# Last layer of a fused four-layer kernel: scores and value mix as three split terms each, with their inputs rounded early in a batch

## The chip, the cores and the metric

The kernel runs on 1 core of one Trainium2 chip. The time is that of the device for one execution of the whole program, in microseconds (us). Lower is better. The change touches the last of three stages of the program; the two stages before it are the same instructions in both kernels.

## What is computed

Four layers act one after the other on `x` of 32 batches, 256 positions and 256 channels. The last two are done in one stage of the kernel, batch by batch, and this is the part of the reference that the change is about:

```
# layer L2: a feed-forward layer with a shared part and an expert chosen per batch
h = gelu(x @ W1 + b1)                       # 256 -> 1024
x = x + concat([h @ W2 + b2, h @ We[indices] + be[indices]], -1)    # 192 + 64 columns
# layer L3: attention of a batch on the tensor `key` (also its value)
q = x + braak_embed[braak_stages][..., None]
attn = softmax(einsum('bsd,btd->bst', q, key), axis=-1)
x = x + einsum('bst,btd->bsd', attn, value)
```

## The kernel before, in words

The whole of `x` stays on the chip, transposed, in `x_all` (128 partitions, 2 chunks of channels, 32 batches of 256 columns). The stage in question is `expert_and_final`, whose tiles and semaphores all begin with `c_`. Each engine has its own instruction list, written out by hand as a `body(n, par, ...)` for batch `n`; batches 2 to 29 run in a hardware loop with two bodies in it (even and odd), and the first two and last two batches are written out. Nothing is scheduled by a planner: the order in each list is the order on that engine, and semaphores tie the lists together.

Matrix products with the feed-forward weights are done in three terms: each operand is split into a rounded part (`_hi`, type fp32r) and the rest (`_lo`, the difference), and high x high, high x low and low x high are summed. The two products of the attention, scores (`c_pS`, L1820) and value mix (`c_pV`, L1837), use plain fp32 operands instead, four matmuls each.

For each batch the work on the engines is this:

- TensorE (PE): `hidden(n+1, r)`, r = 0 to 3, 12 matmuls each into `c_pH`; `output(n, r)`, 12 matmuls each, all into the one accumulator `c_pO`; `scores(n-1)`; four transposes of the probabilities (`turn`, `c_pT`); and `mix_values(n-1)`. The order of a body is hidden 0, scores, output 0, hidden 1, output 1, hidden 2, turn, output 2, hidden 3, output 3, mix.
- ScalarE (ACT): `hidden` (gelu of `c_pH` into `c_hid`), `exps` (exponentials of the scores with the row maximum as bias, and their sums), `turned` (copy of `c_pT`), `high_x` and `expert_high` (rounded parts). Gelu and exponential need different tables, so each batch has two table loads.
- VectorE (DVE): `split` (rounded part and rest of `c_hid`), `maxima`, `normalize`, `low_x`, `residual` (adds `c_pO` to `x_all`), `queries` (adds the embedding), `final` (adds `c_pV` to `x_all`, into `c_y`).
- GpSimd (POOL): `expert_low` (the rest of the expert weights, `c_w2b_lo`, L1611) and the DMA that stores `c_y`.
- SyncE (SP): the loads of expert weights, biases, embedding, key and value for the next batch.

Links that the prediction follows: `output(n, 0)` waits for `residual(n-1)`, since there is one `c_pO`; `residual(n)` waits for `output(n, 3)`; `scores(n)` waits for `queries(n)`; `maxima(n)` for `scores(n)`; `exps(n)` for `maxima(n)`; `mix_values(n)` for `turned(n)`; `split(n, r)` for gelu r of the batch.

Of the kernel before, what the change touches and what calls it, by code (L numbers as in the profile page):

```python
# [1473 lines left out]
def expert_and_final(nc, sem_ctx, ctx, t, X, NB, consts):  # L1474
# [36 lines left out]
    hid_lo = [sb(f"hid_lo{i}", [P, 2, S], F32R) for i in range(ROUNDS)]  # L1511
    query = sb("query", [P, C, S])
    neg_max = sb("neg_max", [P, C])
# [3 lines left out]
    prob_t = sb("prob_t", [P, C, S])  # L1517
# [8 lines left out]
    d_w1, d_b1, d_w2, w_hi, w_lo = (sem(n) for n in ("d_w1", "d_b1", "d_w2", "w_hi", "w_lo"))  # L1526
    xhi_done, xlo_done, ehi_done, elo_done = (sem(n) for n in ("xhi", "xlo", "ehi", "elo"))
    hid_mm, gelu_done, hhi_done, hlo_done, out_mm, x3_done = (sem(n) for n in ("hid_mm", "gelu", "hhi", "hlo", "out_mm", "x3"))
    query_done, s_mm, max_done, exp_done, inv_done, prob_done = (sem(n) for n in ("query", "s_mm", "max", "exp", "inv", "prob"))
    t_mm, pt_done, v_mm, y_done = (sem(n) for n in ("t_mm", "pt", "v_mm", "y"))  # L1530
# [11 lines left out]
    LOADS = 7  # L1542
    block = ctx.enter_context(nc.Block())

# [11 lines left out]
    @block.sync  # L1556
    def _(sp):
        sp.dma_start(w1[:], t["w1"].rearrange("(k p) e -> p k e", p=P)).then_inc(d_w1, 16)
        sp.dma_start(b1[:], t["b1"]).then_inc(d_b1, 16)
        sp.dma_start(w2[:], t["w2"].rearrange("(k p) e -> p k e", p=P)).then_inc(d_w2, 16)  # L1560
        sp.dma_start(expert_i[:], t["expert"]).then_inc(d_in, 16)
        sp.dma_start(stage_i[:], t["stage"]).then_inc(d_in, 16)
        for i in range(2):
            sp.dma_start(b2[i][:, 0:1], t["b2"][0:P]).then_inc(d_in, 16)
            sp.dma_start(b2[i][0:SHARED - P, 1:2], t["b2"][P:SHARED]).then_inc(d_in, 16)
        sp.dma_start(embed_all[:], t["embed"].partition_broadcast(P)).then_inc(d_in, 16)
        sp.wait_ge(d_in, 16 * LOADS)

        def load(n, par):
            at = slice(n, n + 1) if isinstance(n, int) else bass.ds(n, 1)  # L1570
            expert = sp.value_load(expert_i[0:1, at], min_val=0, max_val=EXPERTS - 1)
            stage = sp.value_load(stage_i[0:1, at], min_val=0, max_val=STAGES - 1)
            if not (isinstance(n, int) and n < 2):
                sp.wait_ge(elo_done, n - 1)

            sp.dma_start(we[par][:], t["we"][bass.ds(expert, 1)].rearrange("o p k e -> p (o k) e")).then_inc(d_exp[par], 16)
            if not (isinstance(n, int) and n < 2):
                sp.wait_ge(x3_done, n - 1)
            sp.dma_start(b2[par][SHARED - P:P, 1:2], t["be"][bass.ds(expert, 1)].rearrange("o p f -> p (o f)")).then_inc(d_bias[par], 16)
# [22 lines left out]
    def _(pool):  # L1602
# [18 lines left out]
        loop(pool, body)  # L1621
        store(NB - 1, 1)
# [4 lines left out]
    def _(dve):  # L1627
# [21 lines left out]
        def queries(n, par):  # L1649
            dve.wait_ge(x3_done, n + 1)  # L1650
            dve.wait_ge(d_emb[par], landed(n, par))
            at_least(dve, s_mm, n)
# [56 lines left out]
        loop(dve, body)  # L1709
        maxima(NB - 1)  # L1710
        normalize(NB - 1)
        final(NB - 1, 1)

    @block.scalar
    def _(act):
# [6 lines left out]
        def expert_high(n, par):  # L1722
# [3 lines left out]
            act.activation(w2b_hi[par][:, :, SHARED - P:P], we[par][:], ACT.Copy).then_inc(ehi_done, 1)  # L1726
# [17 lines left out]
        def turned(n):  # L1744
            act.wait_ge(t_mm, n + 1)
            at_least(act, v_mm, n)
            act.activation(prob_t[:], pT[:], ACT.Copy).then_inc(pt_done, 1)

        def body(n, par, ahead, splits, has_3):
            if ahead:  # L1750
                hidden(n + 1, 0)
            if has_3:
                exps(n - 1)
            if ahead:
                hidden(n + 1, 1)
                hidden(n + 1, 2)
            if has_3:
                turned(n - 1)
            if splits:
                high_x(n + 2, par)  # L1760
            if ahead:
                expert_high(n + 1, 1 - par)
                hidden(n + 1, 3)

# [10 lines left out]
        act.wait_ge(d_b1, 16)  # L1775
        for r in range(ROUNDS):
            hidden(0, r)
        expert_high(0, 0)
        loop(act, body)
        exps(NB - 1)  # L1780
# [3 lines left out]
    def _(pe):  # L1784
# [15 lines left out]
        def output(n, par, r):  # L1800
            pe.wait_ge(hlo_done, ROUNDS * n + r + 1)
            if r == 0:
                pe.wait_ge(elo_done, n + 1)
# [10 lines left out]
        def scores(n, par):  # L1814
            pe.wait_ge(query_done, n + 1)
            pe.wait_ge(d_key[par], landed(n, par))
            at_least(pe, exp_done, n)
            for m in range(C):
                for k in range(C):
                    ins = pe.matmul(pS[:, m], query[:, k, m * P:m * P + P], key_t[par][:, k], start=(k == 0), stop=(k == C - 1))  # L1820
            ins.then_inc(s_mm, 1)

        def turn(n):
            pe.wait_ge(prob_done, C * (n + 1))
            at_least(pe, pt_done, n)
# [5 lines left out]
        def mix_values(n, par):  # L1831
            pe.wait_ge(pt_done, n + 1)
            pe.wait_ge(d_val[par], landed(n, par))
            at_least(pe, y_done, n)
            for m in range(C):
                for k in range(C):
                    ins = pe.matmul(pV[:, m], value[par][:, k, m * P:m * P + P], prob_t[:, k], start=(k == 0), stop=(k == C - 1))  # L1837
            ins.then_inc(v_mm, 1)

        def body(n, par, ahead, splits, has_3):  # L1840
            if ahead:
                hidden(n + 1, 1 - par, 0)
            if has_3:
                scores(n - 1, 1 - par)
            output(n, par, 0)
# [3 lines left out]
            if ahead:  # L1849
                hidden(n + 1, 1 - par, 2)  # L1850
            if has_3:
                turn(n - 1)
            output(n, par, 2)
# [3 lines left out]
            if has_3:  # L1857
                mix_values(n - 1, 1 - par)
# [4 lines left out]
        loop(pe, body)  # L1863
        scores(NB - 1, 1)
# [103 lines left out]
```

## Time and profile before

| | |
|---|---|
| time, median of 3 runs | 1984.78 us (1984.0 to 1987.01) |
| profiled execution: its own time, its span | 1988.33 us, 1986.4 us |
| granted TensorE clock over the span, as a share of full | 0.969 |
| busy over the span | PE 93%, DVE 75%, ACT 59%, POOL 33% |
| last stage | from about 1467 us to the end |

The busy shares are means over three stages that have different limits; the stage that the change touches has to be read by itself, in a stretch of it. Matmul records overlap, since they are pipelined: what a group of matmuls costs is read from start to start, not from the duration of a record. The profiled execution took 3.55 us more than the median.

### The profile page before, as it was taken

What the parts mean: (1) busy time and instruction counts of PE and PEld (TensorE: products, weight loads), DVE (VectorE), ACT (ScalarE), POOL (GpSimd) and SP (SyncE); (2) the same over time, 40 slices, a digit from 0 to 9 for tenths busy, and PEclk for the clock granted to TensorE, in tenths of its full rate; (3) what the DMA queues carried; (4) which work ended last, traced back from release to release, by engine and by line L of the source; (5) the groups of instructions that cost most, each with busy time, mean ns of one, the idle gap of its engine ahead of it and who ended that gap; (6) DMA issues with size and microseconds to landing.
All of it is one profiled execution on the core that took longest, in us unless ns stands there. A gap on an engine that the chain in (4) does not pass through costs nothing. (4 is left out here: it accounts for less than half of the span.)

```text
span 1986.4 us, 43323 instructions
## 1 busy us (share of the span) xinstructions
PE 1839.2 (93%) x14542; PEld 1452.8 (73%) x14542; DVE 1485.8 (75%) x2206; ACT 1180.6 (59%) x2458; POOL 664.7 (33%) x655
## 2 busy tenths in 40 slices
PE   5899999999999994499999999999949999999997
PEld 4565555555555552388888888888849999999997
DVE  6888888888888892787878777787736666666664
ACT  1676667666666662366666666666545555555563
POOL 3244444444444442433343434333301111111111
PEclk9999999999999996699999999999979999999998
DMA  3333333333333320100000000000022222222221
GB/s 94 102 125 105 114 116 123 110 109 118 118 119 106 112 94 27 30 1 0 0 0 0 0 0 0 0 0 0 0 91 62 71 71 82 85 71 71 79 88 46
DMA packets 104940, 126.16 MB, mean 64 GB/s; under 512 B 27840, under 2 KB 70464, under 8 KB 104896
## 3 DMA queue, kind: packets, MB, share of 16 engines
q1 hardware_dynamic: 86912, 102.72, 16.3%
q0 software_dynamic: 17408, 22.61, 3.8%
q8 instruction: 25, 0.41, 0.1%
q10 hardware_dynamic: 576, 0.26, 0.1%
q14 instruction: 19, 0.16, 0.0%
HBM read 56.54 MB, written 9.44 MB: 33 GB/s over the span
## 5 line engine op out<-in xcount | busy, mean ns | idle before, releaser
L409 DVE TENSOR_REDUCE a_top<-a_s 128x4 f32<-128x1024 f32 x256 | 309.1, 1209 | 88.5 <-PE a_s L646 88.4
L509 ACT ACTIVATE a_e<-a_t 128x512 f32<-128x512 f32 x512 | 276.6, 592 | 147.7 <-PE a_t L660 143.2
L419 DVE SCALAR_TENSOR_TENSOR a_e<-a_e,a_w_t 128x1024 f32<-128x1024 f32 x256 | 328.1, 1282 | 6.3 <-ACT a_e L509 6.3
L1733 ACT ACTIVATE c_hid<-c_pH,c_b 128x256 f32<-128x256 f32 x256 | 107.4, 471 | 190.1 <-PE c_pH L1796 189.7
L926 POOL TENSOR_TENSOR b_decayed<-b_table,b_mod_t 128x1024 f32<-128x1024 f32 x64 | 118.8, 1876 | 211.3 <-ACT b_mod_t L1198 211.3
L1357 PE MATMUL b_pS<-b_gated_t,b_decayed 128*128 128x256 f32 x768 | 183.8, 389 | 1.0
L675 PE MATMUL a_v<-a_e,a_v_pad 128*32 128x256 f32 x2048 | 165.4, 396 | 8.8 <-DVE a_e L419 6.9
L641 PE MATMUL a_s<-a_absent,a_eye 64*128 64x512 bf16 x1024 | 157.1, 386 | 6.7 <-DMA a_absent<-a_absent 5.4
L1796 PE MATMUL c_pH<-c_x_hi,c_w_hi 128*128 128x256 f32 x512 | 150.8, 294 | 12.5 <-DVE c_w_lo L1698 12.4
L1357 PEld LDWEIGHTS b_pS<-b_gated_t,b_decayed 128*128 128x128 f32 x768 | 142.3, 192 | 23.8 <-issue 6.7
L646 PE MATMUL a_s<-a_st 63*128 63x256 f32 x1024 | 152.5, 377 | 0.0
L1611 POOL TENSOR_TENSOR c_w2b_lo<-c_we,c_w2b_hi 128x512 fp32r<-128x512 f32 x32 | 54.6, 1706 | 280.0 <-ACT c_w2b_hi L1726 280.0
L1796 PE MATMUL c_pH<-c_x_hi,c_w_lo 128*128 128x256 f32 x512 | 146.2, 286 | 0.0
L1796 PE MATMUL c_pH<-c_x_lo,c_w_hi 128*128 128x256 f32 x512 | 145.6, 284 | 0.0
L1065 DVE TENSOR_TENSOR b_inner<-b_inner,b_prod 128x448 f32<-128x448 f32 (+6 forms) x224 | 128.0, 571 | 22.7
L1637 DVE CAST c_hid_hi<-c_hid 128x512 fp32r<-128x512 f32 x128 | 54.5, 426 | 114.6 <-PE c_pO L1810 93.2
L1048 DVE TENSOR_TENSOR b_state<-b_pS,b_w_rep 128x512 f32<-128x512 f32 x128 | 85.3, 687 | 65.5 <-PE b_pS L1357 65.5
L646 PEld LDWEIGHTS a_s<-a_st 63*128 63x128 f32 x1024 | 99.1, 190 | 37.8 <-issue 1.4
L262 POOL TENSOR_TENSOR a_split<-a_full,a_split 128x512 fp32r<-128x512 f32 x64 | 91.8, 1435 | 61.0 <-DVE a_e L419 36.8
L660 PE MATMUL a_t<-a_st 64*128 64x256 f32 x1024 | 108.0, 290 | 4.2 <-ACT a_e L509 2.8
L1796 PEld LDWEIGHTS c_pH<-c_x_hi,c_w_hi 128*128 128x128 f32 x512 | 98.8, 193 | 13.9 <-DVE c_w_lo L1698 12.8
L641 PEld LDWEIGHTS a_s<-a_absent,a_eye 64*128 64x128 bf16 x1024 | 29.4, 95 | 108.1 <-issue 87.7
(253 smaller groups left out, 5152.3 us busy)
## 6 DMA issues: line engine op xcount, KB each, us to landing
a_st<-a_split SPq DMA_DIRECT2D x384, 128.0 KB, 2.2
a_xs<-in_xT SPq DMA_DIRECT2D x32, 256.0 KB, 2.7
x_all<-in_xT SPq DMA_DIRECT2D x32, 256.0 KB, 3.6
a_r_rep<-a_r_rows POOLq DMA_DIRECT2D x64, 128.0 KB, 3.7
c_we<-in_we SPq DMA_DIRECT2D x32, 256.0 KB, 2.7
c_key_t<-in_keyT SPq DMA_DIRECT2D x32, 256.0 KB, 3.2
c_value<-in_key SPq DMA_DIRECT2D x32, 256.0 KB, 2.7
out<-c_y POOLq DMA_DIRECT2D x32, 256.0 KB, 3.3
```

What stands on the lines that cost most here:

```text
L409: dve.tensor_reduce(top[:, qc, half].rearrange("p (r j c) -> p r j c", r=2, j=2)[:, :, cc], ps_s[g % 2][:], AX.X, ALU.max)\
L419: dve.scalar_tensor_tensor(out=buf[:], in0=buf[:], scalar=BIG, in1=w_t[par][:, kc].unsqueeze(1).to_broadcast([P, 4, S]), op0=ALU.min, op1= ...
L509: act.activation(e[g % E_BUFS][:, 2 * r:2 * r + 2], ps_t[r][:], ACT.Exp).then_inc(exp_done, 1)
L641: pe.matmul(ps_s[g % 2][:, r], eye[par][rows, hq], absent2[rows, qc, hq].unsqueeze(1).to_broadcast([64, C, S]), start=(hq == 0), stop=Fals ...
L646: ins = pe.matmul(ps_s[g % 2][:, r, c], st[par][rows, 0, j, c, qc * P:qc * P + P], st[par][rows, 1, j, c], start=False, stop=(c == C - 1), ...
L660: ins = pe.matmul(ps_t[r][:, c], st[par][rows, 1, j, c, kc * P:kc * P + P], st[par][rows, 0, j, c], start=True, stop=True, tile_position=( ...
L675: ins = pe.matmul(ps_v[32 * j:32 * j + 32, cc], v_pad[par][:, kc, 4 * (2 * cc + half) + j], e[g % E_BUFS][:, j], start=(g % 4 == 0), stop= ...
L926: ins = pool.tensor_tensor(decayed[par][:, lo:lo + cnt], table[:, lo:lo + cnt], mod_t[:, k].unsqueeze(1).to_broadcast([P, cnt, TRACES]), A ...
L1065: dve.tensor_tensor(y, y, pr, ALU.add).then_inc(inner_done, 1)
L1357: ins = pe.matmul(pS[q % 2][:, i], decayed[par][:, lo:lo + 4].rearrange("p a d -> p (a d)"), gated_t[par][:, k], start=(k == 0), stop=(k = ...
L1733: ins = act.activation(hid[r % 2][:, i], pH[r][:, i], ACT.Gelu, bias=b1[:, 2 * r + i:2 * r + i + 1])
L1796: ins = pe.matmul(pH[r][:, i], w[:, k, m * P:m * P + P], x[par][:, k], start=(w is w1_hi and x is x_hi and k == 0), stop=(x is x_lo and k ...
```

## The change

Scores and value mix are now done in three terms, like the other products: `product` issues 12 matmuls for each, high x high, low x high and high x low. Their operands have to be split first: key and value into `key_p` and `value_p` (rounded on ACT, rest on POOL), query into `query_p` (rounded on ACT, rest on DVE), and the transposed probabilities into two `prob_t` (rounded on ACT, rest on DVE). The orders of the lists are written anew. On PE the value mix of batch n-2 now stands ahead of `output(n, 0)`, and scores of n-1 behind it. The roundings `high_x`, `high_query` and `high_value` stand at the beginning of ACT's body. On DVE `split(n, 3)` and `low_x` go from the end of a body to the next one's beginning, ahead of `maxima`. The store of `c_y` is one batch later.

```diff
@@ gpsimd
+        def low_key(n, par):
+            pool.wait_ge(load_hi, 3 * n + KEY)
+            pool.tensor_tensor(key_p[par][1][:], key_t[par][:], key_p[par][0][:].bitcast(F32), ALU.subtract).then_inc(load_lo, 1)
+        def low_value(n, par):
...
         def body(n, par, ahead, splits, has_3):
+            low_value(n, par)
+            if not first_two(n):
+                store(n - 2, par)
             if ahead:
+                low_key(n + 1, 1 - par)
                 expert_low(n + 1, 1 - par)
-            if has_3:
-                store(n - 1, 1 - par)
@@ vector
+        def low_query(n):
+            dve.wait_ge(qhi_done, n + 1)
+            at_least(dve, s_mm, n)
+            dve.tensor_tensor(query_p[1][:], query[:], query_p[0][:].bitcast(F32), ALU.subtract).then_inc(qlo_done, 1)
+        def low_prob(n):
+            dve.wait_ge(pthi_done, n + 1)
+            at_least(dve, v_mm, n)
+            dve.tensor_tensor(prob_t[1][:], pT[:], prob_t[0][:].bitcast(F32), ALU.subtract).then_inc(ptlo_done, 1)
...
         def body(n, par, ahead, splits, has_3):
             if has_3:
-                maxima(n - 1)
+                split(n, 3)
+                low_query(n - 1)
+            if splits:
+                low_x(n + 2, par)
             if ahead:
                 split(n + 1, 0)
+            if not first_two(n):
+                final(n - 2, par)
             if has_3:
+                maxima(n - 1)
                 normalize(n - 1)
             if ahead:
                 split(n + 1, 1)
                 split(n + 1, 2)
-            if splits:
-                low_x(n + 2, par)
+            if has_3:
+                low_prob(n - 1)
             residual(n, par)
             queries(n, par)
-            if ahead:
-                split(n + 1, 3)
-            if has_3:
-                final(n - 1, 1 - par)
@@ scalar
         def body(n, par, ahead, splits, has_3):
+            if splits:
+                high_x(n + 2, par)
+            if has_3:
+                high_query(n - 1)
             if ahead:
                 hidden(n + 1, 0)
+            high_value(n, par)
             if has_3:
                 exps(n - 1)
             if ahead:
                 hidden(n + 1, 1)
+                high_key(n + 1, 1 - par)
+                expert_high(n + 1, 1 - par)
                 hidden(n + 1, 2)
...
@@ tensor
+        def product(out, w, x):
+            for m in range(C):
+                for k in range(C):
+                    for i, j in ((0, 0), (1, 0), (0, 1)):
+                        ins = pe.matmul(out[:, m], w[i][:, k, m * P:m * P + P], x[j][:, k],
+                                        start=(k == 0 and i == j == 0), stop=(k == C - 1 and j == 1))
+            return ins
...
         def body(n, par, ahead, splits, has_3):
             if ahead:
                 hidden(n + 1, 1 - par, 0)
+            if not first_two(n):
+                mix_values(n - 2, par)
+            output(n, par, 0)
             if has_3:
                 scores(n - 1, 1 - par)
-            output(n, par, 0)
...
-            if has_3:
-                mix_values(n - 1, 1 - par)
```

On DVE, at the seam of an even and an odd batch in the loop of the kernel before, `queries` is followed by the last split, by `final` (`c_y`) and at once by `maxima` (ISA and REGISTER_ALU rows are register work and waits of the sequencer):

```order
L1674 TENSOR_TENSOR c_y<-c_pV,x_all 128x512
L1659 TENSOR_REDUCE c_neg_max<-c_pS 128x2
L1634 ISA
L1636 REGISTER_ALU
L1637 CAST c_hid_hi<-c_hid 128x512
L1639 TENSOR_TENSOR c_hid_lo<-c_hid,c_hid_hi 128x512
```

The same place of the changed kernel, from the last split of the batch to `maxima`:

```order
L1659 TENSOR_TENSOR c_hid_lo<-c_hid,c_hid_hi 128x512
L1680 TENSOR_TENSOR c_query_lo<-c_query,c_query_hi 128x512
L1649 REGISTER_ALU
L1651 ISA
L1651 TENSOR_TENSOR c_x_lo<-x_all,c_x_hi 128x512
L1654 ISA
L1656 REGISTER_ALU
L1657 CAST c_hid_hi<-c_hid 128x512
L1659 TENSOR_TENSOR c_hid_lo<-c_hid,c_hid_hi 128x512
L1704 ISA
L1704 TENSOR_TENSOR c_y<-c_pV,x_all 128x512
L1689 TENSOR_REDUCE c_neg_max<-c_pS 128x2
```

Between the last split of a batch and `maxima` there stood `final` alone; now there stand `low_query`, `low_x`, the first split of the next batch and `final`.

On POOL, one odd batch in the loop of the kernel before has the rest of the expert weights and a store:

```order
L1610 REGISTER_ALU
L1611 TENSOR_TENSOR c_w2b_lo<-c_we,c_w2b_hi 128x8x64
L1604 REGISTER_ALU
L1606 ISA
L1606 DMA out<-c_y 128x2x256
```

The changed kernel has at this place, for the last two batches (where the rows stand without register work):

```order
L1628 TENSOR_TENSOR c_value_lo<-c_value,c_value_hi 128x512
L1614 DMA out<-c_y 128x2x256
L1624 TENSOR_TENSOR c_key_lo<-c_key_t,c_key_hi 128x512
L1619 TENSOR_TENSOR c_w2b_lo<-c_we,c_w2b_hi 128x8x64
L1628 TENSOR_TENSOR c_value_lo<-c_value,c_value_hi 128x512
```

One tensor operation of POOL per batch became three, two of them back to back. On ACT, the changed kernel has from `high_value` to gelu 2, with the semaphores that a row waits for:

```order
L1793 ACTIVATE c_value_hi<-c_value 128x512 [waits c_v_mm,c_d_val1]
L1775 ACT_TABLE_LOAD [waits c_inv,c_t_mm]
L1775 ACTIVATE c_prob,c_row_sum<-c_pS,c_neg_max 128x256 [waits c_max]
L1775 ACTIVATE c_prob,c_row_sum<-c_pS,c_neg_max 128x256
L1763 REGISTER_ALU
L1767 ACT_TABLE_LOAD [waits c_hlo]
L1767 ACTIVATE c_hid<-c_pH,c_b 128x256 [waits c_hid_mm]
L1767 ACTIVATE c_hid<-c_pH,c_b 128x256
L1784 ISA
L1787 ACTIVATE c_key_hi<-c_key_t 128x512 [waits c_s_mm,c_d_key0]
L1760 ACTIVATE c_w2b_hi<-c_we 128x8x64 [waits c_out_mm,c_d_exp0]
```

The table load of the exponentials does not wait for `maxima` (`c_max`) in either half of the loop; in the kernel before it did in one half of it. Two copies now stand between gelu 1 and gelu 2.

## Rows read from the trace of the kernel before

**Rows 1.** Windows: length, busy PE, PEld, DVE, ACT, POOL; clock, DMA share, GB/s.

```profile
1500.00:1950.00 450.00, 449.84 (x3411) 437.30 (x3410) 285.62 (x502) 249.49 (x501) 70.63 (x58) 1.00 0.26 77
```

**Rows 2.** Chain that ended last, in order of time: start, us, what.

```profile
1652.11 1.73 PE c_pV L1837 x8
1655.26 1.73 PE c_pS L1820 x8
...
1667.39 1.73 PE c_pV L1837 x8
...
1961.53 2.83 PE c_pO L1810 x24
```

**Rows 3.** Timeline of ACT, two batches: start, us, line, what.

```profile
1646.20 0.84 ACT L1733 ACTIVATE c_hid<-c_pH,c_b 128x256 f32<-128x256 f32 x2
...
1657.75 0.47 ACT L1741 ACTIVATE c_prob<-c_pS,c_neg_max 128x256 f32<-128x256 f32 x1 [0.23 <-DVE c_neg_max L1659]
...
1658.78 1.28 ACT L1733 ACT_TABLE_LOAD   x1
1660.08 0.84 ACT L1733 ACTIVATE c_hid<-c_pH,c_b 128x256 f32<-128x256 f32 x2
...
1663.93 0.64 ACT L1720 ACTIVATE c_x_hi<-x_all 128x512 fp32r x1
1664.45 0.64 ACT L1726 ACTIVATE c_w2b_hi<-c_we 128x512 fp32r<-128x512 f32 x1
```

**Rows 4.** Timeline of DVE, the same two batches.

```profile
1647.16 0.43 DVE L1637 CAST c_hid_hi<-c_hid 128x512 fp32r<-128x512 f32 x1 [1.32 <-ACT c_hid L1733]
...
1657.02 0.69 DVE L1659 TENSOR_REDUCE c_neg_max<-c_pS 128x2 f32<-128x512 f32 x1 [1.40 <-PE c_pS L1820]
...
1664.58 0.43 DVE L1637 CAST c_hid_hi<-c_hid 128x512 fp32r<-128x512 f32 x1 [2.14 <-PE c_pO L1810]
1665.04 0.69 DVE L1639 TENSOR_TENSOR c_hid_lo<-c_hid,c_hid_hi 128x512 fp32r<-128x512 f32 x1
1665.65 1.78 DVE L1631 TENSOR_TENSOR c_x_lo<-x_all,c_x_hi 128x512 fp32r<-128x512 f32 x1
1667.54 0.88 DVE L1645 SCALAR_TENSOR_TENSOR x_all<-c_pO,c_b,x_all 128x256 f32 x2
1668.45 0.69 DVE L1654 TENSOR_TENSOR c_query<-x_all,c_embed 128x512 f32<-128x512 f32 x1
```

**Rows 5.** Timeline of POOL: last stage, then the middle stage.

```profile
1665.18 1.71 POOL L1611 TENSOR_TENSOR c_w2b_lo<-c_we,c_w2b_hi 128x512 fp32r<-128x512 f32 x1 [8.16 <-ACT c_w2b_hi L1726]
...
832.25 1.27 POOL L937 TENSOR_TENSOR b_x_lo<-x_all,b_x_hi 128x512 fp32r<-128x512 f32 x1
```

**Rows 6.** Timeline of POOL and DVE, 28 to 32 us; DVE at 832 us.

```profile
28.49 2.56 POOL L262 TENSOR_TENSOR a_split<-a_full,a_split 128x512 fp32r<-128x512 f32 x2 [18.26 <-ACT a_split L485]
...
28.74 1.13 DVE L389 TENSOR_SCALAR a_mix<-a_lam 128x32 f32<-128x32 f32 x1
29.91 1.19 DVE L390 TENSOR_SCALAR a_mix<-a_mix 128x32 f32<-128x32 f32 x1
31.13 0.18 DVE L391 TENSOR_SCALAR a_decay<-a_decay 128x32 f32<-128x32 f32 x1
...
832.63 0.69 DVE L1048 TENSOR_TENSOR b_state<-b_pS,b_w_rep 128x512 f32<-128x512 f32 x1 [1.49 <-PE b_pS L1357]
```

**Rows 7.** Timeline, beginning and end of the last stage.

```profile
1486.87 1.71 POOL L1611 TENSOR_TENSOR c_w2b_lo<-c_we,c_w2b_hi 128x512 fp32r<-128x512 f32 x1 [19.83 <-ACT c_w2b_hi L1726]
...
1975.89 3.78 PE L1837 MATMUL c_pV<-c_prob_t,c_value 128*128 128x256 f32 x8 [0.69 <-ACT c_prob_t L1747]
```

**Rows 8.** Windows of 2 us beside idle time of PE.

```profile
844.00:846.00 2.00, 0.96 (x10) 0.45 (x10) 1.93 (x6) 0.40 (x2) 0.00 (x0) 1.00 0.00 0
1486.00:1488.00 2.00, 0.84 (x8) 0.64 (x6) 1.14 (x3) 1.63 (x4) 1.13 (x1) 1.00 0.65 203
1488.00:1490.00 2.00, 1.27 (x8) 1.30 (x9) 0.00 (x0) 0.00 (x0) 0.58 (x1) 0.81 0.58 167
```

More of the change, by code:

```diff
@@ L1511, in expert_and_final @@
     hid_lo = [sb(f"hid_lo{i}", [P, 2, S], F32R) for i in range(ROUNDS)]
+    key_p = [[sb(f"key_{part}{i}", [P, C, S], F32R) for part in ("hi", "lo")] for i in range(2)]
+    value_p = [[sb(f"value_{part}{i}", [P, C, D], F32R) for part in ("hi", "lo")] for i in range(2)]
     query = sb("query", [P, C, S])
+    query_p = [sb(f"query_{part}", [P, C, S], F32R) for part in ("hi", "lo")]
     neg_max = sb("neg_max", [P, C])
@@ L1516, in expert_and_final @@
     prob = sb("prob", [P, C, S])
-    prob_t = sb("prob_t", [P, C, S])
+    prob_t = [sb(f"prob_t_{part}", [P, C, S], F32R) for part in ("hi", "lo")]
     y = [sb(f"y{i}", [P, C, S]) for i in range(2)]
@@ L1540, in batch_of, with first_two @@
         return src[bass.ds(n, 1)]
-    LOADS = 7
+    LOADS = 8
+    KEY, EXPERT, VALUE = 1, 2, 3
     block = ctx.enter_context(nc.Block())
+    def first_two(n):
+        return isinstance(n, int) and n < 2
     def loop(eng, body):
@@ L1709, in _ @@
         loop(dve, body)
+        low_query(NB - 1)
+        final(NB - 2, 0)
         maxima(NB - 1)
         normalize(NB - 1)
+        low_prob(NB - 1)
         final(NB - 1, 1)
@@ L1725, in expert_high @@
                 act.wait_ge(out_mm, ROUNDS * (n - 1))
-            act.activation(w2b_hi[par][:, :, SHARED - P:P], we[par][:], ACT.Copy).then_inc(ehi_done, 1)
+            act.activation(w2b_hi[par][:, :, SHARED - P:P], we[par][:], ACT.Copy).then_inc(load_hi, 1)
         def hidden(n, r):
@@ L1746, in turned, with high_key, high_value, high_query @@
             at_least(act, v_mm, n)
-            act.activation(prob_t[:], pT[:], ACT.Copy).then_inc(pt_done, 1)
+            act.activation(prob_t[0][:], pT[:], ACT.Copy).then_inc(pthi_done, 1)
+        def high_key(n, par):
+            act.wait_ge(d_key[par], landed(n, par))
+            if not (isinstance(n, int) and n < 2):
+                act.wait_ge(s_mm, n - 1)
+            act.activation(key_p[par][0][:], key_t[par][:], ACT.Copy).then_inc(load_hi, 1)
+        def high_value(n, par):
+            act.wait_ge(d_val[par], landed(n, par))
+            if not (isinstance(n, int) and n < 2):
+                act.wait_ge(v_mm, n - 1)
+            act.activation(value_p[par][0][:], value[par][:], ACT.Copy).then_inc(load_hi, 1)
+        def high_query(n):
+            act.wait_ge(query_done, n + 1)
+            at_least(act, s_mm, n)
+            act.activation(query_p[0][:], query[:], ACT.Copy).then_inc(qhi_done, 1)
         def body(n, par, ahead, splits, has_3):
+            if splits:
+                high_x(n + 2, par)
+            if has_3:
+                high_query(n - 1)
             if ahead:
                 hidden(n + 1, 0)
+            high_value(n, par)
             if has_3:
@@ L1774, in _ @@
         ins.then_inc(w_hi, 1)
-        act.wait_ge(d_b1, 16)
+        act.wait_ge(d_in, 16 * LOADS)
         for r in range(ROUNDS):
             hidden(0, r)
+        high_key(0, 0)
         expert_high(0, 0)
         loop(act, body)
+        high_query(NB - 1)
         exps(NB - 1)
@@ L1831, in mix_values @@
         def mix_values(n, par):
-            pe.wait_ge(pt_done, n + 1)
-            pe.wait_ge(d_val[par], landed(n, par))
+            pe.wait_ge(ptlo_done, n + 1)
+            pe.wait_ge(load_lo, 3 * n + VALUE)
             at_least(pe, y_done, n)
[L1835 to L1838, printed above, removed]
+            product(pV, value_p[par], prob_t).then_inc(v_mm, 1)
         def body(n, par, ahead, splits, has_3):
@@ L1850, in body @@
                 hidden(n + 1, 1 - par, 2)
+            output(n, par, 2)
             if has_3:
                 turn(n - 1)
-            output(n, par, 2)
             if ahead:
@@ L1863, in _ @@
         loop(pe, body)
+        mix_values(NB - 2, 0)
         scores(NB - 1, 1)
```

43 lines of the change are left out of this document (22 added, 21 removed).

## The prediction

> **What bounds the kernel now.** The page's busy shares (the table above) mix three stages, so I went first to the windows of the last one. Over 450 us PE is busy for 449.84 us at full clock [rows 1]: PE never waits, and DVE (285.62 us, 63%) and ACT (249.49 us, 55%) have slack. The chain that ended last says the same: it stays on PE from batch to batch, and one value mix follows the next after 1667.39 - 1652.11 = 15.28 us [rows 2]. That is the period of a batch. A change that takes PE work away can therefore gain only until some other loop through the engines takes 15.28 us too; so I read PE's part from the chain, and the other loop from the timelines of ACT, DVE and POOL.
>
> **What PE saves.** Scores take 1.73 us, the mix 1.73 us (8 records for 4 plain fp32 matmuls) [rows 2]. The new form is 12 matmuls of the kind of `output`, 24 of which take 2.83 us [rows 2], so 12 x 0.118 = 1.42 us. Saved: 2 x 0.31 = 0.62 us a batch. If PE stayed full, the period would be 15.28 - 0.62 = 14.66 us.
>
> **What the other engines get.** ACT: three copies (key, value, query), each 0.52 us from start to start (1664.45 - 1663.93) [rows 3]; 55% of 15.28 us is 8.5 us, plus 1.6 us, so ACT is not full. DVE: `low_query` and `low_prob`, each like `c_hid_lo`, whose successor starts 0.61 us later (1665.65 - 1665.04) [rows 4]. Its sum, 9.7 us plus 1.2 us, also fits. The third addition is what I take to decide: POOL has two more subtractions. Alone such an operation takes 1.27 us [rows 5], but it does not run beside every DVE operation. POOL's `c_w2b_lo` came at 1665.18, while DVE was in `c_hid_lo`; it ended at 1666.89, which is 1.27 us after DVE's next operation could start. That one, `c_x_lo`, took 1.78 us [rows 4] where 0.69 us is its size: it was held for 1.09 us. It is not only for two inputs: a `TENSOR_SCALAR` of 128x32, 0.18 us by itself, took 1.13 and 1.19 us beside two POOL subtractions back to back, one held by each [rows 6]. That row also shows the alternation: DVE gets one operation in between and is held again. A DVE operation with one input in PSUM is not held (832.63, 0.69 us, inside POOL's 832.25 to 833.52) [rows 5, 6]. So casts, `c_hid_lo`, `c_x_lo`, `c_query_lo`, `c_query` are held; `final`, `maxima`, `residual`, `low_prob` are not.
>
> The Trainium skill (SBUF — State Buffer, "Who interferes with whom") says this as a rule: DVE in a two-port mode or with two SBUF inputs and GpSimd exclude each other for a whole instruction. The trace agrees in kind. With the whole 1.27 us as price of a hold where the row has 1.09 us, the sum below would come out 0.5 us a batch longer, 2010 us in all.
>
> **The loop that DVE now closes.** `maxima` is now behind six operations of the kind that is held, and everything after it comes back to them. Start to start, one batch, from [rows 3, 4]: `low_x` 0.61; held by `low_value` 1.10; split 0 1.07 (the cast 0.46, the rest 0.61); `final` 0.61 (taken as `c_hid_lo`, the same size); `maxima` to exponential 0.73; exponential to table load 1.03; table load to gelu 1 1.30; gelu 1 to its cast 0.96 (1646.20 to 1647.16); split 1 1.07; held by `low_key` 1.10; cast of split 2 0.46; held by `expert_low` 1.10; its rest 0.61; `low_prob` 0.61; `residual` 0.91; `queries` 0.61 (the same size again); split 3 1.07; `low_query` 0.61, and `low_x` of the next batch. The sum is 15.56 us. The order of the changed kernel has no other DVE work that could be put between. `normalize` and gelu 2 lie beside it: gelu 2's cast would be ready about 2.8 us after gelu 1 starts (0.84 + 2 x 0.52 + 0.96), the loop brings DVE there after 0.96 + 1.07 + 1.10 = 3.13 us. The holds do fall on it: `low_value` is ready when its copy ends, behind `high_query` and gelu 0 (0.69 + 0.05 + 0.52 + 0.84 + 0.64 = 2.74 us after `queries` starts; the 0.05 us is a hand-off). From the same point DVE has `queries`, split 3 and `low_query` until 2.29 us and `low_x` until 2.90 us, so the split behind it is held; `low_key` is ready 0.96 + 0.46 us after gelu 1 starts, inside split 1, and `expert_low` right behind it. Without any hold the loop would be 12.26 us, less than PE's 14.66 us.
>
> I take 15.6 us (0.04 us for hand-offs): 0.32 us a batch more than before, although PE has less to do. PE would wait about 0.9 us a batch, before the mix (for `c_prob_t_lo`, since DVE is late) and before scores (for `c_query_lo`).
>
> **Beginning and end.** Output 0 of batch 0 started when POOL's `c_w2b_lo` was done (1488.58) [rows 7]; `c_key_lo` is now ahead of it, 1.3 us more. At the end, query rounding and rest stand before the last scores (0.64 + 0.61, 1.2 us), and `low_prob` before the last mix, 0.6 us; the last mix took 3.78 us at half clock [rows 7], 12 short ones would take 2 x 1.42 = 2.8 us there, and the last scores save 0.3 us: 1.2 + 0.6 - 1.0 - 0.3 = 0.5 us more. SP's loads of key and value now wait for POOL's subtraction instead of for PE's products of the batch two before; both are over more than half a batch before the load is wanted, so I give them nothing, and nothing either to the store one batch later, behind which only POOL's own `low_key` stands.
>
> **Sum.** 29 periods x 0.32 = 9.3 us, with 1.3 and 0.5 us: 11.1 us. The profiled execution's 1988.33 us becomes 1999.4 us; it lay 3.55 us above the median, so against the median 1984.78 + 11.1 = 1995.9 us.
>
> **Rivals.**
> - The promised gain: the DVE loop stays under 14.66 us and PE stays full. That needs only one hold less (15.56 - 1.10 = 14.46 us), if `low_value` comes 0.7 us later and falls beside `final` and `maxima`, or a cast can run beside POOL. 29 x -0.62 + 1.8 = -16.2 us: 1968.6 us. For it: the threshold is one hold away. Against it: the row at 28.74 us shows one-input operations held, and the copies are ready early.
> - In between: one hold half hidden (`low_key` beside the wait for gelu 2, 0.4 us). Period 15.2 us, -0.1 x 29 + 1.8 = -1 us: no change.
> - More than the sum: each hold at 1.27 us and each semaphore 0.03 us more, 16.1 us a batch: 29 x 0.82 + 1.8 = +26 us, 2010 us. The same mechanism, its upper bound.
> - The clock: PE fell to half clock after 1.9 us without work (1.16 us in one window, 0.73 us in the next) [rows 8], but not where it was busy for 0.96 of 2 us [rows 8]. The waits I expect are about 0.5 us each. If the clock fell nevertheless, a stretch like that after 1488 us costs some 2 us each time and the kernel would be well above 2010 us.
> - The new form is no cheaper on PE (12 loads of weights against 8). Then PE needs 15.28 us and the DVE loop still decides: the forecast stands.
>
> **How the numbers follow.** A measurement of this kernel tells about 0.2%, 4 us, from no change. The DVE loop with three holds, with its upper bound and the clock: 0.65. In between: 0.13. PE full: 0.22. So slower 0.65, same 0.13, faster 0.22. The likeliest case's own range is 1989 to 2010 us. For 8 in 10 it has to take in the middle case and a part of the fast one, which has its own spread of 1964 to 1980 us: 1973 to 2010 us.
>
> **What will show it.** In a window of 450 us inside the stage PE is busy for 94% and not 100%. `c_pS` and `c_pV` have 12 records each, 1.42 us in all. Two casts `c_hid_hi` of a batch take about 1.5 us instead of 0.43 us (behind `low_value` and `low_key`), and one `c_hid_lo` about 1.8 us (behind `expert_low`). POOL's three rows are 1.3 to 1.7 us. The waits name `c_prob_t_lo` and `c_query_lo` for PE; the exponentials start right after `maxima`. The prediction is wrong if the casts keep 0.43 us, if POOL's rows fall beside `final`, `maxima`, `residual` or idle time, or if the mixes follow each other after 14.7 us.

## The result and the profile after

The changed kernel takes 1990.49 us (median of 7 runs, 1988.27 to 1993.38), the kernel before 1984.78 us (7 runs, 1982.48 to 1987.88): ratio 1.0028, 95% interval 1.0016 to 1.0039. It is slower, by 5.7 us, where 11.1 us were forecast. A second measurement beside further runs of both (below) gave 1989.24 us against 1985.2 us: 4.0 us.

First the window that answers to [rows 1], 1500 to 1950 us, of the changed kernel (length, busy PE, PEld, DVE, ACT, POOL; clock, DMA share, GB/s):

```profile
1500.00:1950.00 450.00, 439.56 (x3635) 429.43 (x3634) 353.02 (x558) 290.17 (x585) 156.43 (x116) 1.00 0.24 77
```

PE is no longer full: 439.56 of 450 us (97.7%). DVE went from 285.62 to 353.02 us, POOL from 70.63 to 156.43 us. No engine but PE looks full in this row, and yet PE waits. The chain that ended last says for what; it answers to [rows 2] (start, us, what):

```profile
1652.55 0.69 DVE c_prob_t_lo L1685
1653.24 0.23 issue
1653.47 1.67 PE c_pV L1875 x12
1655.14 1.42 PE c_pO L1866 x12
1656.55 0.10 issue
1656.65 1.66 PE c_pS L1875 x12
1658.31 1.43 PE c_pH L1852 x12
1659.74 1.37 PE c_pO L1866 x12
...
1667.91 0.69 DVE c_prob_t_lo L1685
1668.60 0.23 issue
1668.83 1.67 PE c_pV L1875 x12
```

Once a batch the chain leaves PE for DVE's `c_prob_t_lo`, and one value mix follows the next after 1668.83 - 1653.47 = 15.36 us, where it was 15.28 us. What this view does not show is why `c_prob_t_lo` comes so late: ahead of it there are only short steps of DVE's sequencer, back to PE's last output product. PE is late twice a batch, which its own timeline shows (the last matmul before each wait and the first one behind it):

```profile
1668.30 0.28 PE L1852 MATMUL c_pH<-c_x_lo,c_w_hi 128*128 128x256 f32 x1
1668.83 0.36 PE L1875 MATMUL c_pV<-c_prob_t_hi,c_value_hi 128*128 128x256 f32 x1 [0.25 <-DVE c_prob_t_lo L1685]
...
1671.63 0.28 PE L1866 MATMUL c_pO<-c_hid_lo,c_w2b_hi 128*128 128x256 f32 x1
1672.01 0.36 PE L1875 MATMUL c_pS<-c_key_hi,c_query_hi 128*128 128x256 f32 x1
```

Matmuls follow each other here after 0.12 us; these two pairs are 0.53 and 0.38 us apart, so PE is 0.41 us late for the mix and 0.26 us for the scores. The loop that sets this is on DVE. Its timeline over one batch, from `low_x` to the next `low_x`, answers to [rows 4]:

```profile
1656.32 0.68 DVE L1651 TENSOR_TENSOR c_x_lo<-x_all,c_x_hi 128x512 fp32r<-128x512 f32 x1
1656.92 1.52 DVE L1657 CAST c_hid_hi<-c_hid 128x512 fp32r<-128x512 f32 x1
1658.48 0.69 DVE L1659 TENSOR_TENSOR c_hid_lo<-c_hid,c_hid_hi 128x512 fp32r<-128x512 f32 x1
1659.09 0.68 DVE L1704 TENSOR_TENSOR c_y<-c_pV,x_all 128x512 f32<-128x512 f32 x1
1659.69 0.68 DVE L1689 TENSOR_REDUCE c_neg_max<-c_pS 128x2 f32<-128x512 f32 x1
...
1663.70 0.43 DVE L1657 CAST c_hid_hi<-c_hid 128x512 fp32r<-128x512 f32 x1 [1.33 <-ACT c_hid L1767]
1664.16 0.69 DVE L1659 TENSOR_TENSOR c_hid_lo<-c_hid,c_hid_hi 128x512 fp32r<-128x512 f32 x1
1665.47 0.82 DVE L1657 CAST c_hid_hi<-c_hid 128x512 fp32r<-128x512 f32 x1 [0.61 <-ACT c_hid L1767]
1666.32 1.66 DVE L1659 TENSOR_TENSOR c_hid_lo<-c_hid,c_hid_hi 128x512 fp32r<-128x512 f32 x1
1667.91 0.68 DVE L1685 TENSOR_TENSOR c_prob_t_lo<-c_pT,c_prob_t_hi 128x512 fp32r<-128x512 f32 x1
1668.51 0.86 DVE L1665 SCALAR_TENSOR_TENSOR x_all<-c_pO,c_b,x_all 128x256 f32 x2
...
1671.68 0.68 DVE L1651 TENSOR_TENSOR c_x_lo<-x_all,c_x_hi 128x512 fp32r<-128x512 f32 x1
```

POOL beside it, which answers to [rows 5]:

```profile
1656.73 1.43 POOL L1628 TENSOR_TENSOR c_value_lo<-c_value,c_value_hi 128x512 fp32r<-128x512 f32 x1 [4.65 <-ACT c_value_hi L1793]
...
1664.19 1.82 POOL L1624 TENSOR_TENSOR c_key_lo<-c_key_t,c_key_hi 128x512 fp32r<-128x512 f32 x1 [2.96 <-ACT c_key_hi L1787]
1665.97 1.47 POOL L1619 TENSOR_TENSOR c_w2b_lo<-c_we,c_w2b_hi 128x512 fp32r<-128x512 f32 x1
```

Read the two together. The cast at 1656.92 takes 1.52 us instead of 0.42 us: it was held by `c_value_lo`, whose row ends at 1658.16 (1656.73 + 1.43), and is over 0.28 us behind that. The rest of split 2, at 1666.32, takes 1.66 us instead of 0.69 us, since `c_w2b_lo` runs until 1667.44. The cast between them is the less plain one: its row shows a wait of 0.61 us for gelu 2 and only 0.39 us more than its size, because `c_key_lo` (until 1666.01) covered the wait as well. From the end of the wait on, everything is back to back until `maxima`; from there the way goes over ACT (exponentials, table load, gelu 1) and back to the cast of split 1.

Where the 3.6 us between the two profiled executions arise can be read from marks that mean the same in both: POOL's last operation of the stage before (L932), and the `residual` rows of batches 0, 2, 29 and 31. Kernel before:

```profile
1465.78 1.26 POOL L932 TENSOR_TENSOR x_all<-b_wsoma,x_all 128x512 f32<-128x512 f32 x1 [15.54 <-ACT b_wsoma L1246]
...
1500.47 0.88 DVE L1645 SCALAR_TENSOR_TENSOR x_all<-c_pO,c_b,x_all 128x256 f32<-128x256 f32 x2
1530.06 0.88 DVE L1645 SCALAR_TENSOR_TENSOR x_all<-c_pO,c_b,x_all 128x256 f32 x2 [0.21 <-PE c_pO L1810]
...
1942.70 0.88 DVE L1645 SCALAR_TENSOR_TENSOR x_all<-c_pO,c_b,x_all 128x256 f32 x2
1967.74 0.88 DVE L1645 SCALAR_TENSOR_TENSOR x_all<-c_pO,c_b,x_all 128x256 f32<-128x256 f32 x2 [3.58 <-PE c_pO L1810]
```

Changed kernel:

```profile
1464.58 1.26 POOL L932 TENSOR_TENSOR x_all<-b_wsoma,x_all 128x512 f32<-128x512 f32 x1 [17.81 <-ACT b_wsoma L1246]
...
1500.19 0.88 DVE L1665 SCALAR_TENSOR_TENSOR x_all<-c_pO,c_b,x_all 128x256 f32<-128x256 f32 x2 [1.62 <-PE c_pO L1866]
1530.23 0.86 DVE L1665 SCALAR_TENSOR_TENSOR x_all<-c_pO,c_b,x_all 128x256 f32 x2
...
1945.07 0.86 DVE L1665 SCALAR_TENSOR_TENSOR x_all<-c_pO,c_b,x_all 128x256 f32 x2
1969.63 0.88 DVE L1665 SCALAR_TENSOR_TENSOR x_all<-c_pO,c_b,x_all 128x256 f32<-128x256 f32 x2
```

| stretch | before, us | after, us | difference |
|---|---|---|---|
| to residual 0 | 34.69 | 35.61 | +0.9 |
| residual 0 to 2 | 29.59 | 30.04 | +0.45 |
| residual 2 to 29 (27 batches) | 412.64 | 414.84 | +2.2 |
| residual 29 to 31 | 25.04 | 24.56 | -0.5 |
| residual 31 to the end of the span | 18.66 | 19.17 | +0.5 |
| sum | 520.6 | 524.2 | +3.6 |

So the loop costs 2.2 / 27 = 0.08 us a batch. How much of this repeats can be seen from a second profiled execution of the changed kernel (from "the changed kernel again", below). It has the same 30.04 us between residual 0 and 2, 414.67 us in the loop and 24.55 us behind it, but 34.06 us up to residual 0 and 19.61 us at the end: -0.6 and +0.95 us against the kernel before. In the 3 us in which the first output products run (from 25 us behind L932) the granted clock was 0.69 before, 0.55 in the first execution of the changed kernel and 1.00 in the second. So the +0.9 us of the first stretch is not a cost that these profiles establish. The medians differ by 5.7 and 4.0 us in the two measurements; the intervals of their ratios, 1.0016 to 1.0039 and 1.0009 to 1.0027, are 3.2 to 7.7 us and 1.8 to 5.4 us, and both hold 3.6 us.

### The profile page after: what moved, and what is told of

It is laid out like the page before. It is cut to its first block and busy times, and to the rows that moved or that the text cites. A ratio compares the mean times of both kernels' runs of the same rounds, so it can differ in the third digit from the quotient of the medians.

```text
span 1988.8 us, 44409 instructions
## 1 busy us (share of the span) xinstructions
PE 1825.5 (92%) x14798; PEld 1444.8 (73%) x14798; DVE 1561.5 (79%) x2270; ACT 1227.7 (62%) x2554; POOL 758.4 (38%) x719
## 3 DMA queue, kind: packets, MB, share of 16 engines
q1 hardware_dynamic: 86912, 102.72, 15.8%
## 5 line engine op out<-in xcount | busy, mean ns | idle before, releaser
L1657 DVE CAST c_hid_hi<-c_hid 128x512 fp32r<-128x512 f32 x128 | 98.8, 772 | 67.0 <-ACT c_hid L1767 60.7
L1659 DVE TENSOR_TENSOR c_hid_lo<-c_hid,c_hid_hi 128x512 fp32r<-128x512 f32 x128 | 119.8, 936 | 4.4
```

The lines of the kernel that those rows point to most:

```text
L1659: dve.tensor_tensor(hid_lo[r][:], hid[r % 2][:], hid_hi[r][:].bitcast(F32), ALU.subtract).then_inc(hlo_done, 1)
```

## The experiments

The theory: a batch lasts as long as the work that DVE does one piece behind the other from `low_x` round to the next `low_x`, three of its operations held by POOL's subtractions, and PE waits for it. Rivals: PE's new order costs the time; ACT's three new copies cost it. Nine runs (eight other kernels, and the changed one again), each timed beside the kernel before (1984.99, 1985.2 and 1985.28 us in the three groups, which ran on different chips). The period of a batch is the mean distance of 26 successive `maxima` rows; PE busy is from 1550 to 1950 us.

| kernel | us, median | ratio to before, 95% | period, us | PE busy of 400 us |
|---|---|---|---|---|
| before | 1984.78 | | 15.29 | 400.00 |
| changed | 1990.49 | 1.0016 to 1.0039 | 15.37 | 390.76 |
| changed, again | 1989.24 | 1.0009 to 1.0027 | 15.36 | 390.58 |
| value's subtraction moved | 1971.18 | 0.9916 to 0.9944 | 14.73 | 399.73 |
| small key | 1969.31 | 0.9904 to 0.9933 | 14.60 | 398.80 |
| both | 1971.05 | 0.9923 to 0.995 | 14.73 | 399.73 |
| extra POOL operation | 2017.38 | 1.015 to 1.018 | 16.34 | 366.73 |
| small x | 1977.32 | 0.9949 to 0.9978 | 14.89 | 395.84 |
| order only | 1981.9 | 0.9976 to 0.9994 | 15.22 | 400.00 |
| split only | 2039.23 | 1.0262 to 1.029 | 16.87 | 356.90 |
| value moved, expert first | 1969.36 | 0.9909 to 0.9936 | 14.73 | 399.73 |

**Value's subtraction moved.** One line of POOL's list goes behind the store, so that POOL waits for `c_y` first and `c_value_lo` falls beside another piece of DVE's work.

```diff
@@ gpsimd body
-            low_value(n, par)
             if not first_two(n):
                 store(n - 2, par)
+            low_value(n, par)
```

> The changed kernel, but POOL stores c_y of batch n-2 before it subtracts for c_value_lo, so that the subtraction waits for final. Nothing is left out. Theory A (a loop on DVE of 15.36 us a batch with three holds by POOL in it decides): c_value_lo falls beside normalize and idle time of DVE, the cast of split 0 goes from 1.52 to 0.43 us, the loop would take 15.36 - 1.09 = 14.27 us, less than the work of PE, and PE sets the period at 14.6 to 14.7 us: 28 x 0.7 = 20 us less, about 1971 us. Theory B (the waits of PE come from its new order: value mix and output 0 stand too close behind residual): the place of a POOL subtraction changes nothing, about 1990 us. Theory C (the two copies on ACT between gelu 1 and gelu 2 are what lengthens the loop): about 1990 us too, since they stay.

Measured 1971.18 us, 18 to 19 us less than the changed kernel. DVE's timeline and POOL's of this kernel:

```profile
1649.45 0.43 DVE L1657 CAST c_hid_hi<-c_hid 128x512 fp32r<-128x512 f32 x1 [0.21 <-PE c_pO L1866]
...
1653.19 1.15 DVE L1697 TENSOR_SCALAR c_prob<-c_prob,c_row_inv 128x256 f32<-128x256 f32 x2
1655.13 0.43 DVE L1657 CAST c_hid_hi<-c_hid 128x512 fp32r<-128x512 f32 x1 [0.80 <-ACT c_hid L1767]
```

```profile
1652.61 1.30 POOL L1628 TENSOR_TENSOR c_value_lo<-c_value,c_value_hi 128x512 fp32r<-128x512 f32 x1
```

The cast of split 0 is back at 0.43 us. POOL now holds `normalize` (1.15 us for two, 0.62 us in the changed kernel), and this costs nothing, because DVE waits for gelu 1 behind it anyway: that wait went from 1.33 to 0.80 us. PE is full again. PE's order and ACT's copies are those of the changed kernel, so both rivals, which gave 1990 us, fall here.

**Small key.** POOL subtracts 16 of key's 256 columns in the loop. This kernel leaves out most of the rest of key there.

```diff
-            pool.tensor_tensor(key_p[par][1][:], key_t[par][:], key_p[par][0][:].bitcast(F32), ...)
+            cols = slice(None) if isinstance(n, int) else slice(0, 16)
+            pool.tensor_tensor(key_p[par][1][:, :, cols], key_t[par][:, :, cols], ...)
```

> The changed kernel, but inside the hardware loop POOL subtracts only 16 of 256 columns for c_key_lo (the rest keeps old values: this part of the result is left out); PE does the same matmuls. Theory A: the hold behind split 1 is that of the expert subtraction now, 0.4 us, and c_hid_lo of split 2 is free (0.69 us, not 1.66): 15.36 - 0.98 = 14.38 us, under PE's work, so 14.6 to 14.7 us a batch and about 1971 us. Theory B and C: no change, about 1990 us.

Measured 1969.31 us, period 14.60 us. DVE's two operations behind gelu 2 in this kernel:

```profile
1659.10 1.03 DVE L1659 CAST c_hid_hi<-c_hid 128x512 fp32r<-128x512 f32 x1 [0.62 <-ACT c_hid L1769]
1660.16 0.69 DVE L1661 TENSOR_TENSOR c_hid_lo<-c_hid,c_hid_hi 128x512 fp32r<-128x512 f32 x1
```

POOL's subtraction for the expert weights now falls on the cast:

```profile
1658.56 1.29 POOL L1619 TENSOR_TENSOR c_w2b_lo<-c_we,c_w2b_hi 128x512 fp32r<-128x512 f32 x1
```

From this cast to the operation behind the rest are 1.67 us (`c_prob_t_lo` starts at 1660.77), against 2.44 us in the changed kernel (1665.47 to 1667.91). The difference, 0.77 us, is that of the periods: 15.37 - 14.60. What the shorter subtraction takes out of DVE's sum is what the period loses. The expectation had the time right and this piece too short: it left 0.4 us of hold on the cast, it is 0.60 us (1.03 - 0.43), and so the sum fell to 14.60 and not to 14.38 us.

**Both of them.**

> The first two experiments together: the subtraction for value moved, and that for key cut to 16 of 256 columns inside the loop (the kernel leaves out most of the rest of key there). If each of them alone had only taken DVE's loop down to TensorE's floor, both together gain nothing more: 14.6 to 14.7 us a batch, 1969 to 1972 us. If DVE's loop still set the time in either, a second hold less would give up to 1.1 us a batch more: 1940 us. Expected 1970 us.

Measured 1971.05 us and 14.73 us a batch. The second hold less gives nothing: what is left is PE. (The two medians are too close to tell this kernel from either of the two before; the periods and PE's busy time do.)

**An extra POOL operation**, a subtraction of the same size behind `low_value` in every batch; it leaves nothing out.

```diff
+        def extra(n, par):
+            if not first_two(n):
+                pool.wait_ge(spare_done, n - 1)
+            pool.tensor_tensor(spare[par][:], w2a_hi[:, 0:4].bitcast(F32), w2a_lo[:, 0:4].bitcast(F32), ALU.subtract)...
@@ body
             low_value(n, par)
+            extra(n, par)
```

> The changed kernel with one subtraction more on POOL per batch, of the same size, into a tile that nobody reads, right behind c_value_lo. Theory A: it holds c_hid_lo of split 0, which takes about 1.7 us; the loop grows by 1.0 to 1.1 us to 16.4 us: 32 x 1.0 = 30 us more, about 2020 us. Theory B and C: POOL is busy for 38% only, no change, about 1990 us.

Measured 2017.38 us; the period grew by 0.97 us. DVE in this kernel, split 0, and POOL beside it:

```profile
1652.16 1.52 DVE L1667 CAST c_hid_hi<-c_hid 128x512 fp32r<-128x512 f32 x1
1653.71 1.67 DVE L1669 TENSOR_TENSOR c_hid_lo<-c_hid,c_hid_hi 128x512 fp32r<-128x512 f32 x1
```

```profile
1652.05 1.35 POOL L1630 TENSOR_TENSOR c_value_lo<-c_value,c_value_hi 128x512 fp32r<-128x512 f32 x1 [4.73 <-ACT c_value_hi L1803]
1653.36 1.48 POOL L1635 TENSOR_TENSOR c_spare<-c_w2a_hi,c_w2a_lo 128x512 f32<-128x512 f32 x1
```

The rest of split 0, 0.69 us in the changed kernel, now takes 1.67 us: 0.98 us, the whole difference.

**Small x.** The same cut on DVE's side: `low_x` subtracts 16 of 256 columns in the loop (most of the rest of x is left out there).

```diff
+            cols = S if isinstance(n, int) else 16
-            dve.tensor_tensor(x_lo[par][:], X[:, :, at], x_hi[par][:].bitcast(F32), ...)
+            dve.tensor_tensor(x_lo[par][:, :, :cols], X[:, :, at], x_hi[par][:, :, :cols].bitcast(F32), ...)
```

> The changed kernel with the rest of the input cut to 16 of 256 columns inside the loop (it leaves out most of the rest of x there), so that DVE has 0.5 us less per batch (0.60 us becomes about 0.1 us) and POOL is left as it is. If the batch is the sum of what DVE does one after the other plus three holds, it falls from 15.36 us by 0.5 us to 14.86 us, just above TensorE's 14.75 us: 28 x 0.5 = 14 us less than the changed kernel, 1975 us (1972 to 1979 us), with the hold of the subtraction for value moved by one operation but as long. If only POOL's operations set the time (the rival: a loop through POOL or through the loads that wait for it), the time stays at 1989 us.

Measured 1977.32 us and 14.89 us a batch, 0.47 us less, with all of POOL's operations in place; `c_value_lo` now holds the rest of split 0 (1.66 us) and no longer its cast (0.43 us). So it is DVE's sum that counts, not a loop through POOL or its loads.

**Order only.** The new order of all lists, with plain fp32 products, as before the change.

```diff
@@ tensor, against the kernel before
+            if not first_two(n):
+                mix_values(n - 2, par)
+            output(n, par, 0)
             if has_3:
                 scores(n - 1, 1 - par)
-            output(n, par, 0)
...
-            if has_3:
-                mix_values(n - 1, 1 - par)
```

> The kernel before (plain fp32 products, no further roundings, one POOL subtraction a batch) in the order of the changed kernel: on PE mix n-2 ahead of output 0 and scores behind it, the transposes behind output 2; on DVE split 3 and low_x at the beginning; on ACT high_x first; store one batch later. Theory A: the DVE loop has one hold and no low_query or low_prob, 15.36 - 1.2 - 1.4 = 12.8 us; PE's 15.28 us decide, as in the kernel before: 1983 to 1986 us. Theory B: PE waits for residual as in the changed kernel, 5 us or more above the kernel before.

Measured 1981.9 us, 3 us less than the kernel before: with plain products the order costs PE nothing. That it costs nothing with split products either was shown by the first experiment, where PE is full in this order. The rival "PE's order" falls.

**Split only.** The reverse: split products and roundings, but the order of the kernel before.

```diff
@@ vector body, against the changed kernel
-                split(n, 3)
-                low_query(n - 1)
...
+                maxima(n - 1)
...
+            if ahead:
+                split(n + 1, 3)
+            low_query(n)
+            if has_3:
+                final(n - 1, 1 - par)
```

> The split products and roundings of the changed kernel with the order of the kernel before: value mix of the batch before at the end of TensorE's body, scores behind the first hidden product, maxima first on DVE, the last split, the rest of the query and the addition of the mix at the end. The rest of the query stands now between the end of the output products and the scores: residual 0.9 us, query 0.6 us, ACT's rounding 0.6 us, the last split 1.1 us and the rest 0.6 us are some 3.4 us, where TensorE has only one mix and one hidden product, 2.8 us, to lie over it; with the holds by POOL on top a batch takes 15.3 to 17.5 us. Expected 16.2 us a batch, 2012 us (1990 to 2045 us): the new order is worth more than the split costs. The rival, that the order was not needed because DVE's sum is what counts, gives the time of the changed kernel, 1990 us.

Measured 2039.23 us and 16.87 us a batch: slower as expected, 27 us above the 2012 us expected and inside the range. DVE's rows, `low_x` to `low_query`, with POOL's `c_value_lo` from 1650.43, `c_key_lo` from 1652.10 and `c_w2b_lo` until 1655.07:

```profile
1650.90 1.79 DVE L1650 TENSOR_TENSOR c_x_lo<-x_all,c_x_hi 128x512 fp32r<-128x512 f32 x1
1652.62 0.68 DVE L1684 TENSOR_TENSOR c_prob_t_lo<-c_pT,c_prob_t_hi 128x512 fp32r<-128x512 f32 x1
1653.22 0.86 DVE L1664 SCALAR_TENSOR_TENSOR x_all<-c_pO,c_b,x_all 128x256 f32 x2
1654.11 1.51 DVE L1673 TENSOR_TENSOR c_query<-x_all,c_embed 128x512 f32<-128x512 f32 x1
```

`c_prob_t_lo` and `residual`, with an operand in PSUM, keep their size beside `c_key_lo`; `c_query`, with two in SBUF, is held for 0.82 us, and `c_x_lo` for 1.10 us. The hold of `c_x_lo` now stands ahead of `c_prob_t_lo` and so of the mix, that of `c_query` on the way from the output products to the scores, and PE waits once before each of the two: 0.9 us each by the view of the waits, 1.1 us each from start to start. The new order is worth 50 us to this split (2039.23 against 1989.24 us).

**The changed kernel again**, beside split only, both and value moved with expert first.

> The changed kernel itself, once more, on the chip of the next three. The theory (a loop of DVE work with three waits behind POOL, 15.36 us a batch against 15.28 us of the kernel before, and a beginning that is 0.9 us longer) gives 29 x 0.08 + 0.9 = 3.2 us above the kernel before from these two terms, with the end up to 1 us more: 1988 to 1990 us. That the first measurement of +5.7 us was partly chance would show as +3 to +4 us here.

1989.24 us, +4.0 us, as expected. The interval, 1.8 to 5.4 us, is too wide to confirm the single terms.

**Value moved, and expert weights ahead of key** in ACT's and POOL's lists. As in the first experiment, `low_value` stands behind the store. Of the kernels that compute everything this one has the lowest median.

```diff
-    KEY, EXPERT, VALUE = 1, 2, 3
+    EXPERT, KEY, VALUE = 1, 2, 3
@@ before the bodies, and in them, on POOL and ACT alike
-        low_key(0, 0)
         expert_low(0, 0)
+        low_key(0, 0)
```

(The expectation says "behind that for the expert weights"; in the list value's subtraction stands behind the store and ahead of both others.)

> The order of the first experiment (the subtraction for value behind that for the expert weights), and besides expert weights ahead of key in ACT's and POOL's lists everywhere, the beginning of the stage too. In the loop TensorE stays the bound, so nothing changes there (14.7 us a batch). At the beginning of the stage the first output product waits for the expert weights' rest alone, not for key's ahead of it: one POOL operation of 1.3 to 1.7 us less. Expected 1971.2 - 1.3 = 1969.9 us (1968 to 1971 us). The rival, that the beginning of the stage is hidden behind the work of the stage before, gives no difference to the first experiment.

1969.36 us. Output 0 of batch 0 starts 22.49 us behind the mark L932 (1485.61 - 1463.12), where the changed kernel needs 23.86 us (1488.44 - 1464.58): 1.4 us less. The eight profiled executions with key ahead of expert weights in this place need 23.8 to 24.5 us, so this part is clear; the median against the first experiment (1971.18 us, another chip) or against "both" (1971.05 us) is not clear of the spread. It is 15.8 us faster than the kernel before (0.9922), and 20 us faster than the changed one.

## Why the prediction was right in its mechanism and wrong in its size

The changed kernel came out 5.7 and 4.0 us above the kernel before, where 11.1 us were forecast.

- **The new bound.** "The loop that DVE now closes" was right, and so were the order, PE's waits and the operations that are held. The chain goes through `c_prob_t_lo`, and four kernels that change DVE's sum (one hold less, another shorter, one more, 0.5 us less work) moved the period by -0.63 (down to PE's floor), -0.77, +0.97 and -0.47 us.
- **The term that failed** is the loop's sum, "I take 15.6 us": it is 15.36 us. Of the 0.24 us, the third hold is 0.12 us: forecast with its rest as 1.10 + 0.61 us, it took 1.59 us (1667.91 - 1666.32), since `c_w2b_lo` starts right behind `c_key_lo` and DVE gets its piece in a little later. The 0.04 us for hand-offs were not there: the durations from start to start already held them. The other 0.08 us are steps a hundredth or two shorter each (0.60 for `low_x`, `final`, `low_prob` and `low_query`, 0.71 for 0.73, 0.89 for 0.91). The first hold was exact (1.52 - 0.42 = 1.10 us). What makes so small an error (1.5% of the sum) so large is that only the difference to 15.28 us counts: 0.32 forecast, 0.08 measured. Times 29 that is 7.0 of the 7.5 us by which 11.1 exceeds the 3.6 us between the two profiled executions.
- **The second hold**, 1.10 us in the sum, comes out as a sum, but only 0.39 us of it is a cost of POOL: the other 0.70 us are wait for gelu 2 (1665.47 against the 1664.77 us at which `c_hid_lo` lets go), which is there with or without `c_key_lo`. That the two together give the 1.10 us of the forecast follows from where `c_key_lo` ends (1666.01). That gelu 2 would be ready about 2.8 us after gelu 1 was right: its cast starts 2.73 us after it (1665.47 - 1662.74). The forecast let DVE come later than that (3.13 us) and took the wait to be covered; it did not ask what would be left of it without the hold. Taking key's subtraction away moved the next one up: it now holds the cast (0.60 for 0.39 us) and no longer its rest (nothing for 0.97 us), 0.39 + 0.97 - 0.60 = 0.76 us. This is why it gave 0.77 us and not 1.1 us.
- **The rule of the Trainium skill** (SBUF — State Buffer, "Who interferes with whom"), that the engines exclude each other for a whole instruction, agrees in kind with every hold here, and with what is not held (`c_prob_t_lo` 0.68 us and `residual` 0.86 us beside `c_key_lo` in the split-only kernel). As a price the row was nearer: 1.10 and 0.98 us, not 1.27 us. (The prediction's "1.27 us after DVE's next operation could start" is 1.24 us by the two rows, 1666.89 - 1665.65; no term rests on it.)
- **Beginning and end.** The 1.3 us are there at the start of output 0: 23.8 to 24.5 us behind L932 (mean 24.1) in the eight profiled executions with `c_key_lo` ahead, 22.4 to 23.0 us (mean 22.6) in the three without (before, order only, expert first), 1.5 us between the means. Up to residual 0 the clock covers it (above). Then come 0.45 us that were not foreseen, up to residual 2, and the last two batches give back 0.5 us; both are the same in the two executions of the changed kernel. The end cost 0.5 us as forecast, but by luck: the scores started 1.4 us later and not 1.2, `c_prob_t_lo` put 0.7 us ahead of the mix and not 0.6, the mix at half clock saved 0.85 us and not 1.0, and what made up for it was that the four transposes ran at full clock, 0.66 us for 1.11 us before. In the second execution they ran at half clock, and the end cost 0.95 us.
- **PE's share and waits.** "94%" is 97.7%. Partly the loop is shorter. Partly PE's own need is 14.73 us and not 14.66 us: with PE full, the chain of the kernel with value moved shows 1.44 us for scores and for mix, not 1.42 us. And the busy share does not see most of a short wait: a matmul's row is 0.28 us long where the next starts after 0.12 us, so 0.16 us of each of the two waits count as busy. Of the "about 0.9 us a batch" 0.41 + 0.26 = 0.67 us are there.
- **The rivals.** "One hold less" was the distance to the promised gain: the first experiment did just that with one moved line and gave -13.8 us against the kernel before, where this rival stood at -16.2 us. The clock did not fall in the loop: 1.00 in the window above. ACT's copies cost nothing in time, since in the first experiment all three are there and PE is full.

## What to carry to other kernels

When a change adds POOL subtractions beside a DVE that works without a pause, draw up DVE's list once round the loop and ask of each POOL operation which DVE operation it will meet: beside one with an operand in PSUM, or one with a long enough wait behind it, it was free here; elsewhere it cost 0.8 to 1.1 us a batch as long as DVE's loop was the bound. If the loop then comes out within a per cent or two of the bound it replaces, the forecast is a difference of two large numbers: state it as "near zero, slower or faster", and look for the one line whose move takes a hold out. A place in a list that looks like a detail can be worth as much as the arithmetic: here one subtraction ahead of a store or behind it made 18 to 19 us, and the split products save PE 0.56 us a batch (15.29 - 14.73), 16 us in 29 batches.

## What was not expected of the hardware

- **A hold is a little less than the POOL operation.** 1.10 us when it comes out of idle time, 0.97 or 0.98 us for the second of two in a row, for a POOL operation of 1.27 us. POOL waits in turn: its rows are 1.82 and 1.47 us beside DVE.
- **PE issues at two paces.** Twelve output matmuls take 1.36 to 1.37 us, in three groups of a batch's four or in more, in the kernels in which PE waits somewhere in the batch (changed, extra, small x, split only, and small key with all but no wait), and 1.41 to 1.42 us where it does not wait in the loop (value moved, both, before). So the kernel with one hold too many to be PE-bound (small key, 14.60 us) has a shorter period than the one with both holds gone (14.73 us). In the order-only kernel, where PE shows no wait, both values occur, 1.37 us in every second batch. So having waited is not the cause, or not the only one. Why is open; it was not tried. PE's floor for the changed kernel is thus not one number: 14.73 us in one pace, at most 14.60 us in the other.
- **The order alone was worth 3 us.** Its period is 15.22 us for 15.29 us, 2.0 us in the 27 batches from residual 2 to 29 (410.67 us for 412.64 us), by those shorter groups. At its end the last mix took 2.01 us at clock 1.00, where the kernel before took 3.79 us at 0.50 behind a wait of the same length (2.67 and 2.68 us). What decided between the two clocks stays open.
